# Windowed attention on one Trainium2 core: softmax reciprocals laid out by two DMA hops through DRAM, and roots by GpSimd's power

## The reference

```
def attn_layer(x, Wqkv, qs, ksc, Wo):           # 16 heads of 64, window 32
    q, k, v = split(x @ Wqkv)
    q = l2norm(q) * qs;  k = l2norm(k) * ksc    # t / max(norm(t), 1e-12)
    q = q * cos * scale + rotate_half(q) * sin * scale
    k = k * cos / scale + rotate_half(k) * sin / scale
    sim = q @ k.T * 8                           # in a window of 32 and the one before
    out = softmax(masked(sim)) @ v
    return out @ Wo
def ffn_layer(x, g, bln, W1, b1, W2, b2):
    xn = (x - mean(x)) / sqrt(var(x) + 1e-05) * g + bln
    a, gate = split(xn @ W1 + b1)
    return a * gelu(gate) @ W2 + b2
for i in range(6):
    x = attn_layer(shift_tokens(x), ...) + x
    x = ffn_layer(shift_tokens(x), ...) + x
```

## Time and profile before

| | us |
|---|---|
| median of three runs | 6057.9 (6055.3 to 6059.1) |
| span of the profiled execution | 6062.1 |
| PE busy | 5372.5 (89%) |
| DVE busy | 4241.2 (70%) |
| ACT busy | 3913.4 (65%) |
| POOL busy | 2700.1 (45%) |

### The profile page before, as it was taken

How to read it: one execution, slowest core, us unless ns; L and a number is a source line. 1 busy time by engine, 2 the same in 40 slices (tenths; PEclk the granted TensorE clock), 3 DMA queues, 4 the chain that set the end, 5 groups by cost and what they waited for, 6 DMA issues and landing times. The chain is left out here.

```text
span 6062.1 us, 121575 instructions
## 1 busy us (share of the span) xinstructions
PE 5372.5 (89%) x41154; PEld 3794.5 (63%) x41154; DVE 4241.2 (70%) x16112; ACT 3913.4 (65%) x11510; POOL 2700.1 (45%) x2578
## 2 busy tenths in 40 slices
PE   7885699999999999997489999999999999697989
PEld 5674366666666666665256666666666666464678
DVE  4453688888888888885378888788888887454522
ACT  2211588888888888884178888888888888222333
POOL 0000556556565565652166656566565665230000
PEclk9996799999999999998599999999999999697999
DMA  0000000000000000000000000000000000000000
GB/s 11 22 1 3 22 1 12 9 12 9 1 15 6 12 9 12 8 1 4 21 1 7 10 6 12 9 12 9 4 13 6 12 8 1 5 2 4 2 29 8
DMA packets 30964, 53.45 MB, mean 9 GB/s; under 512 B 7688, under 2 KB 17168, under 8 KB 29712
## 3 DMA queue, kind: packets, MB, share of 16 engines
q1 hardware_dynamic: 30352, 45.66, 2.4%
HBM read 44.60 MB, written 1.05 MB: 8 GB/s over the span
## 5 line engine op out<-in xcount | busy, mean ns | idle before, releaser
L1784 PE MATMUL bank<-wA,next_rowT 128*128 128x512 f32 x2304 | 1213.7, 629 | 194.6 <-DVE turnB L2129 73.1
L1983 ACT ACTIVATE pairs<-pairs,negmax 128x128 f32<-128x128 f32 (+1 forms) x3072 | 1236.8, 418 | 18.6 <-DVE negmax L2090 17.5
L1960 POOL TENSOR_TENSOR turnA<-raw,ropes 128x512 f32<-128x512 f32 x768 | 968.7, 1271 | 169.3 <-ACT raw L2007 140.4
L2090 DVE CUSTOM_DVE_ANT_0 pairs<-bank,bands,big 128x128 f32<-128x128 f32 (+1 forms) x3072 | 941.7, 364 | 64.6 <-PE bank L1716 61.0
L1967 POOL TENSOR_TENSOR qk<-turnA,turnB 128x512 f32<-128x512 f32 x768 | 975.8, 1271 | 0.0
L1944 POOL COPY spread<-recip 128x256 f32<-128x256 f32 x768 | 305.3, 398 | 1257.8 <-DVE recip L2099 1251.4
L1784 PEld LDWEIGHTS bank<-wA,next_rowT 128*128 128x128 f32 x2304 | 369.6, 190 | 676.7 <-DVE turnB L2129 294.3
L1990 ACT ACTIVATE pairsT<-bank 128x512 f32<-128x512 f32 x768 | 465.9, 607 | 302.2 <-PE bank L1729 301.9
L1983 ACT ACTIVATION_READ_ACCUMULATOR pairs<-pairs,negmax 128x1 f32 x3072 | 625.0, 203 | 0.0
L285 POOL TENSOR_TENSOR rstd<-vareps,neg_half 128x2 f32<-128x2 f32 x56 | 39.0, 696 | 1292.4 <-DVE vareps L256 892.7
L2129 DVE TENSOR_TENSOR turnB<-bank,ropes 128x512 f32<-128x512 f32 x768 | 523.1, 681 | 0.0
(11 more groups left out here) (306 smaller groups left out, 11272.8 us busy)
## 6 DMA issues: line engine op xcount, KB each, us to landing
wA<-in_wt_wqkv SPq DMA_DIRECT2D x72, 256.0 KB, 2.8
wB<-in_wt_wo SPq DMA_DIRECT2D x12, 512.0 KB, 3.5
wC<-in_wt_w SPq DMA_DIRECT2D x12, 341.0 KB, 2.9
wD<-in_wt_w SPq DMA_DIRECT2D x12, 192.0 KB, 2.4
big<-in_e_up SPq DMA_DIRECT2D x1, 2048.0 KB
big<-in_e_down SPq DMA_DIRECT2D x1, 2048.0 KB
scl<-in_wt_scales SPq DMA_DIRECT2D x12, 128.0 KB, 3.1
X<-in_x SPq DMA_DIRECT2D x8, 128.0 KB, 2.5
```

Source lines behind the costliest of these rows:

```text
L1784: pe.matmul(side_bank(i)[:, :], c.next_rowT[:, t * P:(t + 1) * P], wqkv[:, k * 512:(k + 1) * 512], start=True, stop=True).then_inc(s.chunk ...
L1960: g.tensor_tensor(c.turnA[:, m % 2, :].rearrange("p (h d) -> p h d", h=8), c.raw[:, m % 4, :].rearrange("p (h d) -> p h d", h=8), cos, ALU ...
L1983: last = a.activation(tile, tile, ACT.Exp, scale=-1.0, bias=c.negmax[:, 2 * p + side, t:t + 1], accum_out=c.pair_sums[:, p % 4, t, side:si ...
L2090: last = v.tensor_tensor_reduce(c.pairs[:, 2 * (p % 4) + side, AT[t]:AT[t] + SPAN[t]], c.bank[side][:, AT[t]:AT[t] + SPAN[t]], c.bands[:, ...
```

## The change

The reciprocals no longer go over POOL, PE and ACT. DVE's reciprocals (now ordered side before half) are stored by SP to a ring in DRAM, 4 lines of 512 values, where one column of 128 partitions becomes one line. When the store has landed, SP loads them back in two DMAs, each copying one side's 256 values to 64 partitions of `shares`. SP gets a window of its own with a store and two loads a slot; the weight loads are put between the store and the loads, in fixed slots. `pe_shares`, `pool_spread` and `act_copy_shares` go away, and so does the tile `spread`. PE's wait for `ctx_ready` moves from `pe_shares` to `pe_weigh`.

The Newton chains in DVE's slots 2 and 6 go away; POOL takes the clamp and one power of -0.5, ahead of "scale0" and "scale1". DVE's steps in slot 4 wait for POOL's root. The chain stays in the last turn and in the tail of a run.

```diff
+SP_WQKV_SLOTS = {2: (2, 0), 3: (4,), 5: (3, 1), 6: (5,)}
-DVE_RSQRT_SLOTS = {2: 0, 6: 1}
-POOL_SLOTS = {1: ("cos0", "cos1", "add0"), 2: ("cos2", "add1", "cos3", "add2"), 3: ("add3", "scale0"),
-              4: ("cos4", "cos5", "add4"), 5: ("cos6", "add5", "cos7", "add6"), 6: ("add7", "scale1")}
+POOL_SLOTS = {1: ("cos0", "cos1", "add0"), 2: ("cos2", "add1", "cos3", "add2"), 3: ("add3", "root0", "scale0"),
+              4: ("cos4", "cos5", "add4"), 5: ("cos6", "add5", "cos7", "add6"), 6: ("add7", "root1", "scale1")}
...
+    ring = nc.dram_tensor(name + "_ring", (4, 2 * HALVES, P), F32).ap()
...
-        def pe_shares(pe, T, p):
-            pe.wait_ge(s.spread_ready, T * PAIRS + p + 1)
-            if T * PAIRS + p - 1 > T0 * PAIRS:
-
-                pe.wait_ge(s.ctx_ready, T * PAIRS + p - 1)
-            for t in range(HALVES):
-                pe.transpose(c.bank[4 + p % 2][:, S + t * P:S + (t + 1) * P], c.spread[:, p % 2, t * P:(t + 1) * P],
-                             c.ident[:, :])
-
         def pe_weigh(pe, T, p):
             pe.wait_ge(s.probsT_ready, T * PAIRS + p + 1)
             pe.wait_ge(s.prev_ready, T * PAIRS + p + 1)
+            if T * PAIRS + p - 1 > T0 * PAIRS:
+
+                pe.wait_ge(s.ctx_ready, T * PAIRS + p - 1)
...
-        def pool_spread(g, T, p):
...
+        def pool_roots(g, x, y):
+
+            guarded.after(g.tensor_scalar(x, x, 1e-24, None, ALU.max), g)
+            return g.tensor_tensor(y, x, c.neg_half[:, 0:x.shape[-1]], ALU.pow)
...
+                elif item[:4] == "root":
+                    n = 32
+                    if m == 0 and has_turn(q - 3):
+                        g.wait_ge(s.ff_var_ready, q - 2)
+                        n = 32 + HALVES
+                    else:
+                        g.wait_ge(s.chunk_rotated, q * ROTATED + 4 * m + 4)
+                    if q > T0 + 1:
+
+                        g.wait_ge(s.negmax_ready, (q - 1) * PAIRS)
+                    pool_roots(g, ss[:, 34 * m:34 * m + n], rs[q % 2][:, 34 * m:34 * m + n]).then_inc(s.rs_ready, 1)
...
-        def act_copy_shares(a, T, p):
-            a.wait_ge(s.ctx_in_psum, T * PAIRS + p + 1)
-            a.activation(c.shares[:, p % 2, :], c.bank[4 + p % 2][:, S:2 * S], ACT.Identity).then_inc(s.shares_ready, 1)
...
         def dve_share(v, T, p):
-            v.wait_ge(s.shares_ready, T * PAIRS + p + 1)
+            v.wait_ge(s.ctx_in_psum, T * PAIRS + p + 1)
+            v.wait_ge(s.shares_loaded[p % 2], 32 * (T * (PAIRS // 2) + p // 2 + 1))
...
-            step.after(v.tensor_scalar(ss[:, ff_var], ff_mv[:, :, 1], LN_EPS, None, ALU.add), v)
+            v.tensor_scalar(ss[:, ff_var], ff_mv[:, :, 1], LN_EPS, None, ALU.add).then_inc(s.ff_var_ready, 1)
+            v.wait_ge(s.ff_var_ready, f + 1)
...
-            if slot in DVE_RSQRT_SLOTS:
-                g = DVE_RSQRT_SLOTS[slot]
-
-                v.wait_ge(s.chunk_rotated, q * ROTATED + 4 * g + 4)
-                if g == 0 and has_turn(q - 3):
-                    dve_roots(v, ss[:, 0:32 + HALVES], rs[q % 2][:, 0:32 + HALVES])
-                else:
-                    dve_roots(v, norms(ss, g), norms(rs[q % 2], g))
-                v.memset(c.recip[:, 0, 31:32], 0.0).then_inc(s.rs_ready, 1)
...
                 if p == 4 and has_turn(T - 2):
+                    if following:
+                        v.wait_ge(s.rs_ready, (T + 1) * 2 + 1)
                     dve_ff_normalise(v, T - 2, rs[(T + 1) % 2][:, ff_var])
...
+        def sp_store_recip(sp, T, p):
+
+            sp.wait_ge(s.recip_ready, T * PAIRS + p + 1)
+            with nc.allow_non_contiguous_dma(reason="one column of reciprocals becomes one line"):
+                sp.dma_start(ring[p % 4].rearrange("n q -> q n"),
+                             c.recip[:, 0, 4 * (p % 4):4 * (p % 4) + 4]).then_inc(s.recip_stored, 16)
+
+        def sp_load_shares(sp, T, p):
+
+            sp.wait_ge(s.recip_stored, 16 * (T * PAIRS + p + 1))
+            if T * PAIRS + p - 1 > T0 * PAIRS:
+
+                sp.wait_ge(s.ctx_ready, T * PAIRS + p - 1)
+            for side in range(2):
+                sp.dma_start(c.shares[DH * side:DH * side + DH, p % 2, :],
+                             ring[p % 4, 2 * side:2 * side + 2, :].rearrange("t q -> (t q)").partition_broadcast(DH)
+                             ).then_inc(s.shares_loaded[p % 2], 16)
...
+        def sp_window(sp, T):
+            def layer_starts(turn):
+                return T0 < turn < T1 and starts_layer(turn)
+            for p in range(PAIRS):
+                sp_store_recip(sp, T, p)
+                if layer_starts(T + 2):
+                    if p == 0:
+                        sp_scales(sp, T + 2, False)
+                    for k in SP_WQKV_SLOTS.get(p, ()):
+                        sp_wqkv(sp, T + 2, k, False)
+                if layer_starts(T) and p == 7:
+                    sp_wo(sp, T, False)
+                if layer_starts(T - 2):
+                    if p == 0:
+                        sp_w1(sp, T - 2, False)
+                    if p == 1:
+                        sp_cols(sp, T - 2, False)
+                    if p == 3:
+                        sp_w2(sp, T - 2, False)
+                sp_load_shares(sp, T, p)
```

More of the change, by code:

```diff
@@ L130, in allocate @@
     c.probsT = c.pairsT[:, :, :].rearrange("p a b -> p (a b)")[:, 0:1024].rearrange("p (a b) -> p a b", a=2)
-    c.pair_sums = sb("pair_sums", [P, 4, HALVES, 2])
+    c.pair_sums = sb("pair_sums", [P, 4, 2, HALVES])
     c.shares = sb("shares", [P, 2, S])
     c.recip = sb("recip", [P, 2, 32])
-    c.spread = sb("spread", [P, 2, S])
     c.ctx = sb("ctx", [P, HALVES, D])
@@ L1641, in windowed_transformers @@
      s.rowT_in_psum, s.xT_ready, s.chunk_in_psum, s.chunk_copied, s.chunk_squared,
-     s.straight_ready, s.chunk_rotated, s.sum_ready, s.rs_ready, s.keys_scaled,
+     s.straight_ready, s.chunk_rotated, s.sum_ready, s.ff_var_ready, s.norms_guarded, s.rs_ready, s.keys_scaled,
      s.qT_in_psum, s.kT_in_psum, s.qT_copied, s.kT_copied, s.scores_ready, s.scores_seen, s.negmax_ready,
-     s.probs_ready, s.probsT_in_psum, s.probsT_ready, s.prev_ready, s.recip_ready, s.spread_ready, s.ctx_in_psum, s.shares_ready, s.ctx_ready,
+     s.probs_ready, s.probsT_in_psum, s.probsT_ready, s.prev_ready, s.recip_ready, s.recip_stored, s.ctx_in_psum, s.ctx_ready,
      s.out_in_psum, s.shifted_in_psum, s.normed, s.normedT_in_psum, s.normedT_ready,
@@ L1647, in windowed_transformers @@
     wqkv_loaded = [sem(name + "_wqkv_loaded" + str(k)) for k in range(CHUNKS)]
+    s.shares_loaded = [sem(name + "_shares_loaded" + str(n)) for n in range(2)]
     step = Count(steps)
+    guarded = Count(s.norms_guarded)
     wqkv, wo = c.wA[:, :], c.wB[:, :]
     w1, w2 = c.wC[:, :], c.wD[:, :]
+    ring = nc.dram_tensor(name + "_ring", (4, 2 * HALVES, P), F32).ap()
     vn, tn = HALVES * NH * DH, 8 * S
@@ L1983, in act_probs @@
                 last = a.activation(tile, tile, ACT.Exp, scale=-1.0, bias=c.negmax[:, 2 * p + side, t:t + 1],
[L1984 removed]
+                                    accum_out=c.pair_sums[:, p % 4, side, t:t + 1])
             if side == 1:
@@ new lines, in sp_scales, with sp_wqkv @@
+        def sp_scales(sp, T, first):
+            if not first:
+                sp.wait_ge(s.tables_ready, layer_of(T))
+            sp.dma_start(c.scl[:, :, :].rearrange("p a b -> p (a b)"),
+                         w["scales"][layer_of(T)].partition_broadcast(P)).then_inc(s.scales_loaded, 16)
+        def sp_wqkv(sp, T, k, first):
+            if not first:
+                sp.wait_ge(s.chunk_in_psum, (T - 1) * N_CHUNKS + CHUNK_ORDER.index((1, k)) + 1)
+            sp.dma_start(wqkv[:, k * 512:(k + 1) * 512],
+                         w["wqkv"][layer_of(T)][:, k * 512:(k + 1) * 512]).then_inc(wqkv_loaded[k], 16)
@@ new lines, in sp_wo, with sp_w1, sp_cols @@
+        def sp_wo(sp, T, first):
+            if not first:
+                sp.wait_ge(s.out_in_psum, T)
+            sp.dma_start(wo, w["wo"][layer_of(T)]).then_inc(s.wo_loaded, 16)
+        def sp_w1(sp, T, first):
+            if not first:
+                sp.wait_ge(s.linear_in_psum, T)
+            sp.dma_start(w1, w["w1"][layer_of(T)]).then_inc(s.ff_loaded, 16)
+        def sp_cols(sp, T, first):
+            if not first:
+                sp.wait_ge(s.hidden_ready, T * 3)
+            sp.dma_start(c.cols[:, 0:8], w["cols"][layer_of(T)]).then_inc(s.ff_loaded, 16)
@@ new lines, in sp_w2 @@
+        def sp_w2(sp, T, first):
+            if not first:
+                sp.wait_ge(s.ff_out_in_psum, T)
+            sp.dma_start(w2, w["w2"][layer_of(T)]).then_inc(s.w2_loaded, 16)
+        def sp_window(sp, T):
[18 more added lines that the diff above has]
+                sp_load_shares(sp, T, p)
@@ L2272, in _ @@
                 sp.dma_start(c.rope[:, :, :, 0:DH], w["rope"]).then_inc(tables_loaded, 16)
[L2273 to L2299, removed]
-                        sp.wait_ge(s.ff_out_in_psum, T)
```

(18 more changed lines are left out.)

22 lines of the change are left out of this document (3 added, 19 removed).

## The result

The changed kernel takes 9908.9 us (median of 4 runs, 9898 to 9924), the kernel before on the same chip 6058.5: a ratio of 1.636, 95% interval 1.634 to 1.638. The forecast was 5826 us.

A forecast was written before the change was run, and what follows sets the result against it. PE was taken as the bound, 94% busy. Gains of 1.76 and 1.08 less 0.3 of wait gave -2.54 us a turn, times 96 = -244, plus 12 for edges: -232, so 5826 us; range 5720 to 6000.

The forecast's parts named there:

- (e): Reciprocals' round trip through DRAM: store lands after 2.5 us (2.0 to 4.1), SP's cycle 3.5 us a pair, hidden, cost 0.
- the estimate of about 2.0 us: Store's landing by the Trainium skill's fixed DMA cost, set beside the forecast's own 2.5 us.
- Rival A: Store too slow, SP sets the pace above a 5.58 us cycle: 6380 to 6770 us; chance 0.13.
- (a): PE loses two transposes of the spread a pair, 0.22 us: 1.76 us a turn gained at full value.
- (b): DVE loses two Newton chains a turn; PE's stops for late rotation and key copies go: 1.08 us a turn gained.
- (c): ACT loses the copy of the shares, POOL the spread; neither bounds, so 0.
- (d): POOL gets two roots a turn, 5.8 and 5.5 us; DVE's slot 4 normalisation waits 0.3 us a turn.
- rival B: POOL's loop to scale 1 (39.8 us against a 42.1 turn) sets the turn, gain cut: about 5930 us; chance 0.15.
- Rival D: Shared port: a DVE instruction beside POOL's 5.8 us root stops up to 5.8 us a turn: 6380 us; chance 0.02.
- (f): Edges of the two runs, last pair's open round trip and first turn's slower roots: 12 us in all, 0 to 25.

The follow-up runs named there:

- store_16B: The changed kernel, but each partition's four reciprocals are stored as one 16-byte piece, so the loads read them in the wrong order: 5898 us.
- newton_hold: The changed kernel with 16-byte store pieces (wrong order), Newton chains back on DVE, POOL's sum 3 held until group 0's norms are ready: 6021 us (0.993).

## Why the prediction was wrong, point by point

**The step that failed is (e), the store.** It was put at 2.5 us, at most 4.1, from the landing of a small read (1.6) and the time that packets take. SP's wait and issue are 9.05; the estimate of about 2.0 us that stood beside it was as far off. The rest of (e) held: a load takes 3.6 us to land, as taken, and 0.54 to issue. The packets were no worse than thought; what the bound left out is the time from the last packet to the landing, 5.8 us without any traffic, which depends on how the short pieces lie to each other. The bound was none: it priced a part of the landing by rows in which that part hardly exists. The row for the read of 32-byte pieces says nothing of writing, and an upper bound of four times 1.6 us, 6.4, was at hand and would itself have been too low.

**Rival A was the right mechanism, at 0.13**, with the right place and the right point of decision (SP's cycle above 5.58 us), and a price a fifth of the real one: SP's cycle is 10.2 us, 81 us a turn. The 3 us a turn that are missing to 84.4 lie in SP's queue too, and not in PE's lower clock: over 690 to 4740 us a store waits 8.56 us in the mean, two loads take 1.23 to issue, the layers' weights 31 us in all, and SP waits but 19 us for reciprocals. The range ended at 6000 and left it out. With a step that has no row and a cliff 0.5 us above its bound, A deserved a third of the chance, and the range its price.

**With a cheap store** the rest of the sum can be read from store_16B: 5898 us against 5826. The same instruction recurs there after 44.37 - 1.59 = 42.78 us:

```profile
2001.59 0.42 DVE L2146 TENSOR_TENSOR Y<-Y,bank 128x256 f32<-128x256 f32 x1 [4.64 <-PE bank L1815]
...
2044.37 0.42 DVE L2146 TENSOR_TENSOR Y<-Y,bank 128x256 f32<-128x256 f32 x1 [4.63 <-PE bank L1815]
```

That is 1.86 us a turn instead of 2.54.

(a) Per pair the two transposes were indeed 0.22 us of PE's queue: from the last L1731 to L1718 are now 0.20 us, before 0.42. But "at full value" held only together with the roots on POOL: with the chains on DVE a turn is 44.22 us (newton_hold), so (a) alone gives 0.42 of its 1.76.

(b) It was the wrong size, and of its two stops one didn't go. PE's waits from 700 to 2640 us in store_16B:

```profile
PE bank L1780 <- DVE turnB L2119: 39.2, 46, 1.0
PE bank L1730 <- ACT pairs L1981: 19.0, 44, 0.5
```

The key copies (0.45 us a turn) are gone as forecast; the rotation has grown from 0.63 to 0.86 a turn, though no chain is left: by the program's order it hangs on PE's own chunk over ACT and DVE. That is 0.22 gained, not 1.08, on top of (a)'s 1.76; less the 0.14 that (c) lost it makes 1.84, against 1.86 measured. DVE's chain was worth more than its stops in the profile, because a shorter PE runs into it.

(c) held nearly: ACT and POOL don't bind, but PE's stop for the exponentials, ahead of which ACT loads a table for 1.28 us, has grown from 0.29 us a turn (13.5 us in 47) to 0.43.

(d) held: 5.84 and 5.45 us for the powers (5.8 and 5.5), 0.29 for the guard (0.3). DVE never waited for the root at the normalisation, where 0.3 was taken. POOL's loop (rival B) didn't bind. Rival D was right on the port as a mechanism, in a place that it didn't name: not beside the root but beside a sum, in kernels with the chain still there. The rule of SBUF — State Buffer (the Trainium skill), SBUF: two separate sides, agrees with 0.18 against 1.21 us.

(f) 5898 is 18 us above 6058.5 - 96 x 1.86; 12 were taken.

## What to carry to other kernels

Price a DMA by its landing, and for a store of short pieces look at how they fall in DRAM, not at how many they are: transpose on an engine first, so that each place is written by few long pieces. Where a step without a row in the trace stands close to a cliff, measure it alone before building on it, or give the cliff the chance that the missing row deserves. When work leaves the bounding engine, ask whether the next engine has room for the shorter period, and which idle wait kept two engines off one port.

## What the hardware showed that was not expected

512 writes of 4 bytes side by side in DRAM, sixteen in each 64 bytes: 8.5 us of waiting; the same 512 pieces 64 bytes apart: 1.6 us. In the slow store the traffic ends 5.8 us before the landing, and loads behind the store land 6.8 us later than before (9.6 instead of 2.8). DMA: Bandwidth & Descriptors (the Trainium skill), Rules for kernel authors, advises against a store of single elements; here single elements cost 8.5 us packed and 1.6 us apart, so in this kernel it was their neighbourhood and not their number that counted.
